# Two transformer blocks on one core: the second attention's probabilities with keys on the partitions

## The chip, the cores and the metric

The kernel runs on one core of a Trainium2 chip. The core has five engines that each work through their own queue in order: TensorE (PE) multiplies, with its weight loads shown apart as PEld; VectorE (DVE) and ScalarE (ACT) do element-wise work; GpSimd (POOL) does a little element-wise work here; SyncE (SP) issues DMAs. They meet by semaphores. The metric is the device time of one execution in microseconds; lower is better.

## What is computed

A batch of 2 sequences of 2048 rows by 512 passes through four stages, each with a layer norm and a residual; the context is 77 rows by 512 for each sequence.

```python
# stage 1: attention without heads over the 77 context rows
align = softmax(ex @ eother.T); x = x + tanh(g) * (align @ iother)
# stage 2: feed-forward with ternary weights, 512 -> 2048 -> 512, exact gelu
# stage 3: the second attention: 16 heads of 32, 77 keys
q = query @ Wq + bq; k, v = context @ Wkv + bkv
scores = einsum('bhid,bhjd->bhij', q, k) * 32 ** -0.5
scores = where(mask, -inf, scores)
out = einsum('bhij,bhjd->bhid', softmax(scores), v) @ Wout + bout
# stage 4: gated feed-forward with weights and inputs quantised to fp4 blocks
```

The change touches stage 3 alone, and the order of the work that runs beside it.

## The kernel before

The 4096 rows are taken in 8 groups of 512 (`GROUPS`), each of 4 tiles of 128 rows (`TILES`). Two groups are always in flight. `phase_a(g3, g1)` runs stage 3 of one group beside stage 1 of the next and the first 8 of its 16 up-projections ("ups", L1251) of stage 2. `phase_b(g, s4)` runs the rest of stage 2 of the next group, and its stage 3 queries, beside stage 4 of the first. So the kernel is: phase A and B of group 0 alone, seven periods of A and B with two groups each, and a last phase A with stage 3 alone followed by a last stage 4. A phase is a list of steps (A) or slots (B), written out for each engine: every engine has a function `attend(g, n)` that says what it does for stage 3 at step n of phase A, and `stage1(g, n)` for stage 1. Nothing is planned at run time: an engine takes its queue in this order and waits (`want(engine, name, group, count)`) where a semaphore isn't there yet. An operation that waits holds back all behind it on its engine.

Precision: an fp32 operand is split into a high and a low fp16 half, and a product takes three passes (high by high, high by low, low by high). The low half is made by a subtraction.

Stage 3 of a tile t has 4 chunks c of 4 heads; n = 4t + c is the step. For each chunk:

- PE `scores` (L1329): queries are the weights (128 features by 128 rows), keys of four heads stand side by side as a block-diagonal of 308 columns; three passes and one for the mask, into bank 4 or 5. The result has rows on partitions.
- DVE `row_max` (L967, L969): minus the maximum of each row and head.
- ACT `powers_of` (L543, L550): exp for each head by itself, 128 rows by 77 keys, with minus the maximum as bias, and the sum of the row as a by-product (an `ACTIVATION_READ_ACCUMULATOR` behind each).
- PE, two steps on (L1370): four transposes in fp32, so that keys are on the partitions, into bank 6 or 7. ACT copies the high half out (L561), DVE subtracts to make the low half (L988).
- PE, four steps on: 12 short products with the values into bank 2 (`vals1`).

For each tile: DVE takes the reciprocals of the sums (L993) and normalises into `on3` (L979); PE transposes it (L1380), ACT and DVE split it (L570, L998), PE multiplies by Wout (12 + 1 matmuls, `out3`), DVE adds the residual (L1005) and takes the statistics of stage 4 (L731). When tiles 0 and 1 are there (`VAR4_AT`), POOL takes a root (`root4`, L422, `rstd4`) and DVE normalises and quantises them as the input of stage 4 (`x4`, L914, then `quant_x4` in parts 0 to 4); tiles 2 and 3 follow at the start of phase B.

The scores of steps 0 and 1, their maxima and the first exp are made at the end of phase B, between the third and the fourth query chunk. The fourth quarter of the previous hidden tile is quantised around there as well: its last part (`quant4` part 4) comes in step 2 (`LATE_QUANT`), its transposing DMA from SP after it (`turn_h`, L354), and its down-projection `late_down` (L1308) in steps 4 to 7.

Stage 1 starts its four tiles at steps 0, 1, 6 and 7 (`START1`). Its output is normalised at step 16 (`NORM2_AT`) and transposed by PE at step 17 (`x_t(2, ...)`, L1207, L1220) into banks 0, 1, 4 and 5; ACT makes the high half (L490), DVE the low half (L768); ups 0 to 7 follow in steps 18 to 25. After each up ACT makes gelu twice and a square (L514, L517, L519) and POOL the low half (L443), in its phase B list.

## Time and profile before

| | us |
|---|---|
| median of 3 runs | 1691.92 |
| lowest and highest | 1691.38, 1700.05 |
| the profiled execution | 1697.49 |
| its span, first to last instruction | 1695.7 |
| PE busy | 1348.8 (80%) |
| DVE busy | 1365.5 (81%) |
| ACT busy | 702.5 (41%) |
| POOL busy | 265.1 (16%) |

The seven periods repeat closely. The one looked at below has the end of its phase B (queries) at 808 to 823 us, phase A from 823 to 898, and the next phase B from 898 on. In the chain of work "issue" is time without a releaser that the profile shows. A duration in the timeline includes the time in which the next instruction of the same engine already runs, so what one costs its engine is the distance between two starts.

### The profile page before, as it was taken

What the parts mean: (1) busy time and instruction counts of PE and PEld (TensorE: products, weight loads), DVE (VectorE), ACT (ScalarE), POOL (GpSimd) and SP (SyncE); (2) the same over time, 40 slices, a digit from 0 to 9 for tenths busy, and PEclk for the clock granted to TensorE, in tenths of its full rate; (3) what the DMA queues carried; (4) which work ended last, traced back from release to release, by engine and by line L of the source; (5) the groups of instructions that cost most, each with busy time, mean ns of one, the idle gap of its engine ahead of it and who ended that gap; (6) DMA issues with size and microseconds to landing.
All of it is one profiled execution on the core that took longest, in us unless ns stands there. A gap on an engine that the chain in (4) does not pass through costs nothing.

```text
span 1695.7 us, 22446 instructions
## 1 busy us (share of the span) xinstructions
PE 1348.8 (80%) x8120; PEld 700.3 (41%) x8120; DVE 1365.5 (81%) x2364; ACT 702.5 (41%) x2113; POOL 265.1 (16%) x205
## 2 busy tenths in 40 slices
PE   5053645889988998889889988899889988898775
PEld 4021213644454445434554445344644464344421
DVE  6998688877888787878887788688887888786786
ACT  2222303752365326641565146522763165514510
POOL 1102200032003300230014000320032002400000
PEclk9557867999999999999999999999999999998987
DMA  9264684034113231133103420341132310341012
GB/s 350 90 225 142 133 212 108 2 62 75 50 26 57 44 87 26 32 59 82 29 14 63 75 63 14 62 75 50 26 57 44 88 26 12 62 73 30 20 19 62
DMA packets 267429, 119.71 MB, mean 71 GB/s; under 512 B 244122, under 2 KB 244634, under 8 KB 265782
## 3 DMA queue, kind: packets, MB, share of 16 engines
q1 hardware_dynamic: 259158, 102.54, 26.7%
q10 hardware_dynamic: 8160, 15.73, 2.5%
q8 instruction: 65, 1.06, 0.3%
q14 instruction: 46, 0.38, 0.1%
HBM read 49.04 MB, written 8.39 MB: 34 GB/s over the span
## 4 chain that ended last, share of the span: by engine, by line
PE 41%; DVE 29%; ACT 5%; issue 4%; DMA 1%; POOL 1%; DVEq 0%; POOLq 0%; ACTq 0%
PE bank L1180 23%; PE bank L1280 8%; PE bank L1265 6%; DVE stats L731 3%; DVE amax L884 2%; DVE xt L768 2%; DVE pair L893 2%; DVE region L988 2%; PE bank L1370 2%; DVE hid L937 2%; ACT region L550 1%; PE bank L1313 1%; DVE pair L901 1%; DVE xb L914 1%; DVE pair L903 1%
## 5 line engine op out<-in xcount | busy, mean ns | idle before, releaser
L1265 PE MATMUL bank<-w_up,xt 128*128 128x512 fp8e4 x1024 | 246.9, 393 | 51.7 <-ACT region L517 37.3
L1280 PE MATMUL bank<-w_dn,region 128*128 128x512 fp8e4 x1024 | 235.9, 384 | 29.9 <-DMA region<-region 29.9
L443 POOL TENSOR_TENSOR region<-g,region 128x512 f16<-128x512 f32 x128 | 169.7, 1331 | 265.3 <-ACT region L517 257.4
L532 ACT ACTIVATE th<-bank,each 128x512 f32<-128x512 f32 x100 | 68.7, 687 | 331.0 <-PE bank L1180 322.9
L1265 PEld LDWEIGHTS bank<-w_up,xt 128*128 128x128 f16 x1024 | 102.3, 101 | 178.9 <-ACT region L517 38.3
L1180 PE MATMUL bank<-w_gate,xqt 128*128 128x512 bf16 x512 | 144.0, 407 | 36.0 <-DVE th L926 21.6
L550 ACT ACTIVATE region<-bank,nm 128x77 f32<-128x77 f32 x512 | 159.6, 338 | 21.7 <-DVE nm L969 20.5
L1280 PEld LDWEIGHTS bank<-w_dn,region 128*128 128x128 f16 x1024 | 101.4, 99 | 155.3 <-DMA region<-region 30.9
L1180 PE MATMUL bank<-w_gup,xqt 128*128 128x512 bf16 x512 | 140.6, 399 | 26.0 <-DVE hid L937 20.7
L514 ACT ACTIVATE g<-bank 128x512 f32<-128x512 f32 x128 | 76.4, 597 | 196.3 <-PE bank L1265 178.2
L1220 PE MATMUL bank<-ident,region 128*128 128x128 f32 x384 | 60.7, 310 | 81.6 <-DVE region L762 76.2
L490 ACT ACTIVATE xt<-bank 128x512 f16<-128x512 f32 x96 | 54.9, 605 | 158.8 <-PE bank L1220 158.7
L937 DVE TENSOR_TENSOR hid<-th,bank 128x512 f32<-128x512 f32 x92 | 63.0, 685 | 68.8 <-PE bank L1180 68.2
L550 ACT ACTIVATION_READ_ACCUMULATOR region<-bank,nm 128x1 f32 x512 | 112.1, 219 | 0.0
L561 ACT ACTIVATE region<-bank 77x512 f16<-77x512 f32 x128 | 77.5, 606 | 74.6 <-PE bank L1370 74.3
L1180 PE MATMUL bank<-w_down,hqt 128*128 128x512 bf16 x384 | 91.0, 392 | 13.5 <-DMA hqt<-pair 13.5
L1180 PE MATMUL bank<-w_o,region 128*128 128x512 f16 x384 | 91.1, 388 | 13.2 <-DVE region L998 13.2
L1180 PEld LDWEIGHTS bank<-w_gate,xqt 128*128 128x128 bf16 x512 | 48.6, 102 | 107.1 <-ACT th L532 32.2
L1180 PE MATMUL bank<-xt,w_q 128*128 128x512 f16 x384 | 89.2, 387 | 3.9 <-DVE xt L768 3.1
L1180 PEld LDWEIGHTS bank<-w_gup,xqt 128*128 128x128 bf16 x512 | 48.8, 103 | 105.2 <-DVE hid L937 41.8
L1220 PEld LDWEIGHTS bank<-ident,region 128*128 128x128 f32 x384 | 50.4, 159 | 95.5 <-issue 58.3
L1370 PE MATMUL bank<-ident,region 128*77 128x128 f32 x512 | 86.9, 295 | 2.1 <-DVE x L951 2.1
(211 smaller groups left out, 2525.1 us busy)
## 6 DMA issues: line engine op xcount, KB each, us to landing
out_x<-x ACTq DMA_DIRECT2D x16, 512.0 KB, 2.8
xin<-in_x ACTq DMA_DIRECT2D x14, 512.0 KB, 4.7
region<-in_w_up_t SPq DMA_DIRECT2D x1, 4096.0 KB, 14.0
hid<-in_gate_w SPq DMA_DIRECT2D x4, 1024.0 KB, 5.3
x<-in_gate_w SPq DMA_DIRECT2D x4, 1024.0 KB, 5.6
hid<-in_up_w SPq DMA_DIRECT2D x4, 1024.0 KB, 5.2
x<-in_up_w SPq DMA_DIRECT2D x4, 1024.0 KB, 5.7
hid<-in_down_w SPq DMA_DIRECT2D x4, 1024.0 KB, 4.9
```

Of the source, the lines that this page charges most:

```text
L443: eng.tensor_tensor(hn[1][:, t % 2, ns], g32[:, s % 2, :], hn[0][:, t % 2, ns], ALU.subtract).then_inc(sg["hl"], 1)
L490: eng.activation(xt[0][:, :, t * P:(t + 1) * P], state_bank(stage, t)[:, :].rearrange("p (k t) -> p k t", k=KD), ACT.Copy).then_inc(sg[f"x ...
L514: eng.activation(g32[:, s % 2, :], bank[s % 2][:, :], ACT.Gelu).then_inc(sg["g32"], 1)
L532: eng.activation(th[:, u % 2, :], bank[4][:, :], ACT.Silu, scale=cg[:, :]).then_inc(sg["th"], 1)
L550: last = eng.activation(p3[:, n % 2, j, :], bank[4 + n % 2][:, j * M:(j + 1) * M], ACT.Exp, bias=nm3[:, n % 2, j:j + 1], accum_out=rs3[:, ...
L561: eng.activation(pt3[0][0:M, m % 2], bank[6 + m % 2][0:M, :].rearrange("p (h t) -> p h t", h=HC), ACT.Copy).then_inc(sg["p3h"], 1)
L937: eng.tensor_tensor(buf[:, n * D:(n + 1) * D], th[:, u % 2, :], bank[5][:, :], ALU.mult).then_inc(sg["hid"], 1)
L1180: last = mm(out, lhs, rhs, start=(n == 0), stop=(n == len(pairs) - 1))
L1220: last = tr(state_bank(stage, t)[:, k * P:(k + 1) * P], xn[:, t, k * P:(k + 1) * P], ident[:, :])
L1265: last = mm(bank[s % 2][:, :], xt[i][:, k, ts], w_up[:, k, n * D:(n + 1) * D], start=(k == 0 and i == 0), stop=(k == KD - 1 and i == 1))
L1280: last = mm(bank[2 + t % 2][:, :], ht[i][:, t % 2, f, :], w_dn[:, f, :], start=(f == 0 and i == 0), stop=(f == KF - 1 and i == 1))
L1370: last = tr(bank[6 + m % 2][0:M, j * P:(j + 1) * P], p3[:, m % 2, j, :], ident[:, :])
```

## The change

Stage 3 no longer transposes its probabilities; it makes them with keys on the partitions. This needs each row's maximum before the exponent, on the other axis, so that the scores are made twice.

- Queries and keys of each head are stacked three times 32 rows high (high, high, low against high, low, high), so that one pass over 96 rows takes the place of three: `qs` and `kst`. The stacking is done by DMAs from SP: `stack_q`, 24 DMAs of 64 KB for each group, in two halves of 12 with their own semaphores; it stands between `turn_h(g, 2)` and `turn_h(g, 3)` in SP's list. The keys are stacked once by 12 DMAs.
- First pass, `scores`: the mask (308 columns) and four products of 77 columns, always into bank 4, so it waits for the maxima of the step before. The maxima of a tile (`nm3`) are copied once more beside themselves (`nmc`), transposed by PE in one operation (`turn_max`), and split by ACT and DVE into `mx`.
- Second pass, `shifted_scores`, 5 steps later (`LAG_S`): for each head keys as weights (77 columns), 128 rows moving, and a short product that adds minus the maximum; into bank 6 or 7.
- ACT `powers_of`: two exps over 77 by 512 in place of four exps, four accumulator reads and a copy. The mask of a key is now a bias column `mcol`.
- The low half of the probabilities is made by POOL (`low3`) in place of DVE.
- `weigh`: values carry a column of ones, so that the sums come out of the product; 12 matmuls as before, into two banks. Normalising is done in two halves for each tile.
- Nothing of stage 3's scores is done in phase B any more. `stack_q` waits for the query halves there.
- Order: `LATE_QUANT` goes from step 2 to 0, `late_down` from 4..7 to 3..6. The stage 2 transposes use banks 0 and 1 alone, in steps 17 and 18, and ups 0 to 7 go from steps 18..25 to 19..26. The output of a tile comes later: for tile t the product with Wout goes from step 4t + 11 to 4t + 14. `VAR4_AT` goes from 17 to 20. POOL's low halves of ups 0 to 7 and its roots are now in phase A's list by step, and `root4(g, 1)` is at the head of phase B, behind the low half of up 7 (before: behind that of up 6).

```diff
-LATE_QUANT, LATE_DOWN, LATE_OUT = 2, (4, 5, 6, 7), 8
+LATE_QUANT, LATE_DOWN, LATE_OUT = 0, (3, 4, 5, 6), 7
-UP_AT = {T2_AT + 1 + i: i for i in range(UPS_A)}
+UP_AT = {T2_AT + 2 + i: i for i in range(UPS_A)}
+LAG_MX, LAG_S = 1, 5
+LAG_V = LAG_S + 2
+LAG_ON, LAG_OT, LAG_OTL, LAG_OUT, LAG_X3 = (LAG_V + i for i in (1, 2, 3, 4, 5))
+VAR4_AT = NC + NC - 1 + LAG_X3 + 1
...
+            def stack_q(g):
+                want_ht(sp, g, 2)
+                want_ht(sp, g, 3)
+                for a in range(2):
+                    cs = slice(2 * a, 2 * a + 2)
+                    for r, made, i in ((0, "qh", 0), (1, "qh", 0), (2, "ql", 1)):
+                        want(sp, made, g, 2 * a + 2)
+                        for j in range(HC):
+                            dst = qs[HD * r:HD * (r + 1), :, :].rearrange("p (c j) t -> p c j t", j=HC)[:, cs, j, :]
+                            sp.dma_start(dst, qt[i][HD * j:HD * (j + 1), cs, :]).then_inc(sg[f"stacked{a}"], 16)
...
+                for n in range(STEPS):
...
+                    if g3 is not None and 0 <= n - LAG_S < TILES * NC:
+                        low3(g3, n - LAG_S)
+                    if g3 is not None and n == VAR4_AT:
+                        root4(g3, 0)
+                    if g1 is not None and n in UP_AT:
+                        low(g1, UP_AT[n])
...
-                for j in range(HC):
-                    h = HC * c + j
-                    last = eng.activation(p3[:, n % 2, j, :], bank[4 + n % 2][:, j * M:(j + 1) * M], ACT.Exp,
-                                          bias=nm3[:, n % 2, j:j + 1], accum_out=rs3[:, t % 2, h:h + 1])
-                last.then_inc(sg["p3"], 1)
+                want(act, "s3", g, m + 1)
+                if m >= 2:
+                    want(act, "p3l", g, m - 1)
+                eng.activation(p32[0:M, m % 2, :], bank[6 + m % 2][0:M, :], ACT.Exp, bias=mcol[:, b:b + 1])
+                if m >= 2:
+                    want(act, "o3", g, m - 1)
+                eng.activation(pt3[0][0:M, m % 2, :], bank[6 + m % 2][0:M, :], ACT.Exp,
+                               bias=mcol[:, b:b + 1]).then_inc(sg["p3"], 1)
...
-                elif s < 2:
-                    want(pe, "xl2", g, s + 1)
+                elif s < 2:
+                    want(pe, "xl2", g, s + 3)
...
-                product(bank[4 + n % 2][:, 0:HC * M],
-                        [(qt[0][:, c, sl], k_hi), (qt[0][:, c, sl], k_lo), (qt[1][:, c, sl], k_hi),
-                         (row_one_b[:, :], mrow[:, b].rearrange("p h m -> p (h m)"))]).then_inc(sg["sc3"], 1)
+                if n:
+                    want(pe, "nm3", g, n)
+                at = bank[4]
+                mm(at[:, 0:HC * M], row_one_b[:, :], mrow[:, b].rearrange("p h m -> p (h m)"), start=True, stop=False)
+                for j in range(HC):
+                    last = mm(at[:, j * M:(j + 1) * M], qs[:, HC * c + j, t * P:(t + 1) * P],
+                              kst[:, HC * c + j, b * M:(b + 1) * M], start=False, stop=(j == HC - 1))
...
+            def shifted_scores(g, m):
...
+                if c == 0:
+                    want(pe, "ml", g, t + 1)
+                if m >= 2:
+                    want(pe, "p3", g, m - 1)
...
+                    last = product(bank[6 + m % 2][0:M, j * P:(j + 1) * P],
+                                   [(kst[:, h, b * M:(b + 1) * M], qs[:, h, t * P:(t + 1) * P]),
+                                    (sel[0:MXR, h:h + 1].to_broadcast([MXR, M]), mx[0:MXR, t % 2, :])])
...
+            def weigh(g, m):
...
+                want(pe, "p3l", g, m + 1)
...
+            def attend(g, n):
+                t = tile_at(n, LAG_MX)
+                if t is not None:
+                    turn_max(g, t)
+                if n < TILES * NC:
+                    scores(g, n)
+                if 0 <= n - LAG_S < TILES * NC:
+                    shifted_scores(g, n - LAG_S)
+                if 0 <= n - LAG_V < TILES * NC:
+                    weigh(g, n - LAG_V)
```

## Rows read from the trace of the kernel before

**Rows 1.** Busy time of each engine (instructions) in three stretches: us, engines, granted clock, DMA
```profile
823.40:834.00 10.60, 6.33 (x54) 5.21 (x53) 10.39 (x15) 7.12 (x33) 0.00 (x0) 0.69 0.17 32
834.00:871.40 37.40, 33.65 (x374) 23.64 (x372) 31.20 (x77) 27.30 (x130) 2.33 (x2) 1.00 0.07 21
871.40:906.40 35.00, 28.13 (x158) 13.82 (x158) 27.62 (x54) 21.34 (x47) 13.59 (x12) 0.99 0.37 69
```

**Rows 2.** Chain that ended last, same period: start us, us, engine, tile, line
```profile
843.71 0.59 DVE region L988
...
897.64 1.16 POOL region L443
...
899.49 1.84 DVE xb L914 x2
...
905.71 0.69 DVE th L926
```

**Rows 3.** Timeline of PE: start us, us, line, out<-in, shape, count, idle and releaser
```profile
829.69 0.96 PE L1180 MATMUL bank<-keys,xt 128*128 128x77 f16 x12 [4.27 <-DVE xt L768]
...
847.02 0.59 PE L1180 MATMUL bank<-keys,xt 128*128 128x77 f16 x12
847.45 0.20 PE L1180 MATMUL bank<-crow,row_one 128*128 128x77 f16 x1
...
859.99 0.56 PE L1180 MATMUL bank<-keys,region 128*128 128x308 f16 x3
860.39 0.29 PE L1180 MATMUL bank<-mrow,row_one_b 128*128 128x308 bf16 x1
860.52 0.46 PE L1180 MATMUL bank<-vals,region 77*128 77x32 f16 x12
860.82 0.64 PE L1370 MATMUL bank<-ident,region 128*77 128x128 f32 x4
861.30 0.60 PE L1380 MATMUL bank<-ident,acc 128*128 128x128 f32 x4
...
871.47 2.02 PE L1220 MATMUL bank<-ident,region 128*128 128x128 f32 x16 [0.83 <-DVE region L762]
```

**Rows 4.** Timeline of ACT, and for L538 min/median/max ns of one
```profile
817.98 0.68 ACT L540 ACTIVATE region<-bank,bq 128x512 f16<-128x512 f32 x1
...
821.27 1.28 ACT L550 ACT_TABLE_LOAD   x1
822.57 0.33 ACT L550 ACTIVATE region<-bank,nm 128x77 f32<-128x77 f32 x1
...
822.88 0.32 ACT L550 ACTIVATE region<-bank,nm 128x77 f32<-128x77 f32 x1
...
L538 ACT ACTIVATE region<-bank,bq x32: 687/688/707, 281.5 to 1549.4; 128x512 f32<-128x512 f32 x32
```

**Rows 5.** DVE: two lines with min/median/max ns, then two of its timeline
```profile
L988 DVE TENSOR_TENSOR region<-bank,region x128: 674/677/686, 295.1 to 1590.8; 77x512 f16<-77x512 f32 x128
...
L969 DVE TENSOR_REDUCE nm<-bank x128: 455/469/480, 288.6 to 1585.3; 128x4 f32<-128x308 f32 x128
...
877.52 1.00 DVE L914 TENSOR_SCALAR xb<-x,mv,rstd 128x512 f32<-128x512 f32 x2
...
889.28 0.68 DVE L998 TENSOR_TENSOR region<-bank,region 128x512 f16<-128x512 f32 x1
```

**Rows 6.** SP issuing DMAs at the start; a store with us to landing
```profile
0.72 0.45 SPq L269 DMA_DIRECT2D xb<-in_ctx_t  x1
1.23 0.49 SPq L269 DMA_DIRECT2D region<-in_w_t  x1
...
out_x<-x ACTq DMA_DIRECT2D x16, 512.0 KB, 2.8
```

**Rows 7.** POOL's L443 and DVE's L914: min/median/max ns of one
```profile
L443 POOL TENSOR_TENSOR region<-g,region x128: 1149/1159/2136, 142.5 to 1477.9; 128x512 f16<-128x512 f32 x128
...
L914 DVE TENSOR_SCALAR xb<-x,mv,rstd x32: 533/540/1373, 339.4 to 1610.3; 128x512 f32<-128x512 f32 x32
```

297 lines of the change are left out of this document (152 added, 145 removed).

## The prediction

> **What bounds the kernel now.** I read the busy times first, then the chain of waits, then the timelines of one period, then single lines. PE and DVE are each busy four fifths of the span, ACT well under half. The stretch from the end of the queries to the first gate product that waits for quantised work (823.4 to 906.4 us) is what the change edits. Its windows [rows 1] show three regimes. In the first 10.6 us DVE is busy 10.39 and PE 6.33, at a granted clock of 0.69, so partly at 1.2 instead of 2.4 GHz after it had idled. In the next 37.4 PE (33.65) and DVE (31.20) are both nearly full and ACT has 27.30. In the last 35.0 PE (28.13) and DVE (27.62) hand over to each other. The chain [rows 2] says who ends last: in the middle it changes between PE and DVE, and the low half of the probabilities (L988) lies on it; near the end it goes low half of an up (POOL), root, x4 on DVE from 899.49, hidden tile at 905.71, and PE's gate product at 906.44. So ACT, which the change relieves most, ends last almost nowhere. What counts is PE, DVE and the hand-overs.
>
> **What each step costs its engine.** PE: from the distances of starts [rows 3] three score passes take 0.40 us and the mask 0.13; the 12 value products 0.30; four transposes 0.48; together 1.31 for each of 16 steps. After: the mask 0.13 and four products of 77 columns, which cost 0.036 each where 12 took 0.43 [rows 3], so 0.28 for the first pass. The second pass is 8 products of 128 columns, half of them 48 rows deep, with 77 columns of weights. No row shows these in fp16. From below they cost 0.036 each (the 77-column products), from above 0.12 each (the transposes of the same two sizes, in fp32), so 0.29 to 0.96; I take 0.43, 0.053 each: 128 columns at the rate at which the 308 columns took 0.13. Values 0.30 as before. Sum 1.01, and 4 times about 0.12 for `turn_max`: PE saves 4.3 us a period, 1.0 of it in phase B.
>
> DVE: L988 leaves, 16 times 0.60 (0.677 with 0.08 of overlap) [rows 5], 9.6 us. The halves of the normalising, copies of maxima and the low half of `mx` add some 0.6 a tile. Net 7 us less. `row_max` stays at 0.47 [rows 5], but PE now waits for it in every step, since bank 4 is the only one. ACT: four exps at 0.31 apart [rows 4] and a copy (1.7 us) become two exps of 77 by 512 with a bias column. Bounds: 0.33 [rows 4] and 0.69, a 128 by 512 one with a bias column (L538) [rows 4]; I take 0.6, so 1.2 and 16 times 0.5 us less. POOL: 16 new low halves of 77 by 512; nearest is L443, 1.16 us at the median [rows 7]: 18.6 us more on an idle engine.
>
> **The sum, as a walk through one period.** Times are those of the period before; what is said of after is shifted to the same start.
>
> Start. The second query chunk's high half is there at 818.66 [rows 4]. From then SP can issue. Two issues at the start of the kernel are 0.51 apart [rows 6]; 24 need 12.2 us, so the last of the second half goes out at 830.4. A landing takes up to the 2.8 us of a 512 KB store [rows 6]; nothing says that 64 KB are much quicker, so `stacked1` is there at 833.2 (bounds 831, no time but the issue, and 836, a crowded queue). Queued behind it on PE, in step 2: the scores, then stage 1's first scores, then all else. Those started at 829.69 before, after PE had waited 4.27 us for DVE [rows 3]. After: 833.5. **3.8 us lost**; the old 4.27 us covers the rest. `turn_h(g, 3)` now stands behind 24 issues on SP, but its data is made at about 830, so it leaves at 831, as before, and `late_down` waits at most 1 us.
>
> Middle, up to the stage 2 transposes, which start at 871.47 [rows 3]: 41.8 us before. After, PE's work from step 2 to 16 is 25.6 us: 0.28 a step, 0.43 from step 5, 0.30 from step 7, stage 1, `late_down`, and one product with Wout (2.9 us) where there were two: the other now comes behind the transposes. DVE has 24 us. Taking in each step the longer of the two gives 32; perfect overlap gives 26. The engines run about a step apart, so I take 30.5: transposes at 864.0, **7.5 us earlier**.
>
> Tail, first part. The second product with Wout now lies between the two pairs of transposes (to 869.6), and the second pair uses banks 0 and 1 again, so it waits for DVE's low halves: 870.4. On ACT the copies of that pair stand ahead of the exp of chunk 13, so exps 13 and 14 end at 873.6. Then up 0 wants gelu and chunk 15 wants exp: a table is loaded for gelu, for exp and for gelu again, 1.28 us each [rows 4], where one load did. Load and three operations of up 0, 3.2 us; load and two exps, 2.5: 879.2. On POOL the low half of chunk 15 (1.16) and then the root of tiles 0 and 1 are queued behind it: 881.1. The first half of x4 begins on DVE at 881.2 instead of 877.52 [rows 5]. **So 3.7 later**, though the transposes were 7.5 earlier: ACT, no limit before, becomes one through its order.
>
> Rule against row: the trace has the next exp 0.02 us behind the load's end [rows 4], so a load costs 1.28. The Trainium skill ("ScalarE: Activation LUTs", What ACT_TABLE_LOAD costs) gives about 1.38 us of draining beside it, 2.66 in all. By it two more loads would cost 2.8 us more a period, 19 us in the kernel; the row decides and the sum is without it.
>
> Tail, second part. From there DVE works without a pause to the low half before the last product with Wout (L998, 889.28 [rows 5]): 11.8 us before, now 1.2 more since the last part of the quantising goes ahead of it: 894.2. Product 2.8, up 7 1.7: 898.7. Its second gelu 1.2, low half 1.16, root 0.7: x4's second half at 901.7 instead of 899.49 [rows 2]. Before, the root stood behind up 6's low half, so an up more is now ahead of it. The 7 us from there to PE's gate product are DVE's and do not change: 908.7 instead of 906.44. **2.2 us later a period.** The 1.0 us saved on PE in phase B is in this, since phase A starts that much earlier.
>
> To this come frictions, bounded by 0 and 4 us a period. The clock: PE is idle in two long pieces before 833, and the slow stretch of 4.5 us after the old one cost some 2; I take 0.7. POOL against DVE: x4's L914 takes 540 ns at the median and 1373 at most [rows 7], the latter beside POOL's low halves; 16 more of these now run beside the stage 2 normalising (four wide operations and some small ones) and the copies of maxima; I take 0.6. Weights of 77 columns at the upper bound would add up to 0.5 a step, much of it under DVE. Sum 3.5 a period.
>
> Kernel: 7 times 3.5 is 24.5. The last phase A has no ups, so no second table load, and keeps the gain of the middle: 3.8 - 7.5 + 0.7, 3.0 less. The prologue's key splitting gets shorter on DVE, but DVE waits there next for the sums of the ternary weights, so I count nothing; if that cover is thin it is 1 to 5 us of gain. Together 21.5 more: 1697.5 + 21.5 = 1719.0 for the profiled execution; it lies 5.6 above the median, so the median goes from 1691.9 to **1713.4**.
>
> **The rivals.** (1) ACT's order does not hold the tail. If exp 15 and the root are done by 875, when the statistics of tile 1 are, the tail runs by PE alone: 28.4 us of work from 864 and 1.5 of waits, up 7's end at 893.9 instead of 898.0, and after the extra low half still 3 us before the old time. Seven periods and the last phase: 24 less, 1668. For it: ACT has 13 us of idle in the last window [rows 1]; against it: its queue is in order. This is the other side, and it decides by whether the first x4 starts before about 878.
>
> (2) The terms cancel: the middle comes out at 27 instead of 30.5 or the stacking lands at 831. Within 8 us of the old time, about 1692. For it: L988 lay on the chain [rows 2] and is gone altogether.
>
> (3) The new short loops fail to overlap: one bank for the first pass makes PE and DVE alternate (0.28 + 0.47 and two hand-overs in every step), and POOL's low halves block DVE's wide operations and are blocked. Then the middle takes 34.5, x4 is hit too, 7.5 a period: 52 - 3, 1741. For it: the 1373 and 2136 ns [rows 7]. By the Trainium skill ("SBUF — State Buffer", on the port pair that VectorE and GpSimd share) the later of the two stands still for the other's whole instruction.
>
> **How the numbers follow.** Forecast 0.35 (by itself 1700 to 1727), rival 1 0.25, rival 2 0.18, rival 3 0.22. The range goes from rival 1 to rival 3, 1668 to 1742, since neither can be left out. About 0.5% (8.5 us) is what a measurement of this kernel can tell from no change. Faster by more 0.27, within 0.18, slower by more 0.55.
>
> **What would show it.** In the new trace: SP's 24 issues 0.5 apart and stage 1's first scores at 10 us behind the queries' end or later (right), or at 7 (wrong). The stretch from those to the stage 2 transposes near 30 us. Five table loads a period instead of three. x4's first half waiting for POOL's root, not for its statistics. x4's second half behind up 7's low half. Second-pass products near 0.05 apart. L914 and the stage 2 normalising longer than 0.54. If DVE is still full from the transposes to x4, the forecast of the tail is wrong; if DMA landings are not what PE waits for in step 2, that of the start is.

## The result, and the profile after

| | before | after |
|---|---|---|
| median, us | 1691.65 | 1922.73 |
| lowest and highest | 1688.60, 1700.05 | 1920.95, 1924.73 |
| the profiled execution's span | 1695.7 | 1922.9 |
| PE busy | 1348.8 (80%) | 1533.8 (80%) |
| DVE busy | 1365.5 (81%) | 1318.5 (69%) |
| ACT busy | 702.5 (41%) | 664.8 (35%) |
| POOL busy | 265.1 (16%) | 408.4 (21%) |

The ratio is 1.136, 95% interval 1.132 to 1.139 (four runs each): 13.6% slower, where 1713.4 (1668 to 1742) was forecast. The sign was right, the size was not. The kernel before, run again beside the experiments, had medians of 1690.8 to 1698.0, so a difference of under some 7 us between two kernels says little by itself. DVE, ACT and POOL moved about as expected; PE, which was to become 4.3 us lighter in each period, was busy for 185 us more in all.

The chain that ended last, after:

```profile
PE 52%; DVE 24%; SPq 7%; ACT 6%; issue 5%; DMA 3%; POOL 2%; DVEq 0%; POOLq 0%; ACTq 0%
```

The costliest groups that are new (busy us, mean ns, idle time before and its releaser):

```profile
L1232 PE MATMUL bank<-mx,sel 48*77 48x128 bf16 x512 | 141.4, 276 | 0.0
L1232 PE MATMUL bank<-qs,kst 96*77 96x128 f16 x512 | 139.9, 273 | 0.0
...
L1385 PE MATMUL bank<-mrow,row_one_b 128*128 128x308 bf16 x128 | 49.4, 386 | 83.5 <-DMA qs<-region 82.4
```

The first two lines are the second pass. Their busy times can't be added, since the products overlap; by the starts, a step's eight products hold PE for 1.64 us on average, 210 us in all 128 steps, where 0.43 a step, 55 us, was forecast. The third is where PE waits for the stacked queries, 82.4 us in all.

Windows of one period after (from the queries' end to the first gate product):

```profile
512.10:525.60 13.50, 3.54 (x24) 2.70 (x24) 8.06 (x10) 3.74 (x5) 0.00 (x0) 0.82 0.49 107
525.60:575.40 49.80, 49.11 (x423) 30.77 (x420) 29.21 (x76) 20.90 (x46) 16.09 (x14) 0.74 0.07 20
575.40:595.10 19.70, 19.23 (x143) 11.22 (x144) 9.77 (x21) 12.59 (x21) 6.43 (x6) 0.83 0.00 1
595.10:613.50 18.40, 16.32 (x79) 7.49 (x77) 13.03 (x27) 12.09 (x29) 8.44 (x7) 1.00 0.37 69
```

The second line is the stretch from stage 1's first scores to the stage 2 transposes. The same stretch, in the same period, of the kernel before and of k96, an experiment below:

```profile
469.60:511.40 41.80, 37.41 (x410) 26.73 (x411) 35.59 (x84) 30.00 (x144) 2.33 (x2) 0.97 0.11 27
503.50:539.40 35.90, 31.60 (x422) 23.28 (x419) 27.91 (x76) 20.77 (x46) 16.28 (x15) 0.88 0.10 27
```

After the change PE is busy there for 49.11 of 49.80 us and the granted clock is 0.74, where it was 0.97. DVE has 29.21: it is not the limit there. PE alone sets this stretch, and it does so with the second pass, whose products start 0.178 us apart at 2.4 GHz and 0.25 at 1.2 (timeline of PE: start, us, line, tile):

```profile
539.42 0.25 PE L1232 MATMUL bank<-qs,kst 96*77 96x128 f16 x1
539.61 0.25 PE L1232 MATMUL bank<-mx,sel 48*77 48x128 bf16 x1
539.78 0.25 PE L1232 MATMUL bank<-qs,kst 96*77 96x128 f16 x1
...
559.25 0.33 PE L1232 MATMUL bank<-qs,kst 96*77 96x128 f16 x1
559.50 0.32 PE L1232 MATMUL bank<-mx,sel 48*77 48x128 bf16 x1
```

Where the 227.2 us between the two spans lie, by the starts of PE's queries: 9.8 before the first (276.2 to 286.0), 39.8 in the first phase A and B with two groups (172.3 to 212.1), 153.2 in the six periods that follow (181.0 to 206.5), 24.4 in the last phase A and stage 4 (161.5 to 185.9). The forecast had priced the first period like the six, at 3.5, the prologue at nothing and the last phase at 3.0 less.

To compare kernels I cut the six periods at the same five events and take means. The columns: from the last query product to the first scores of stage 1; from there to the root of stage 2's variances (POOL, `sdev`); from there to the first half of x4; from there to the first gate product; from there to the last query product of the next period (phase B with its queries). This table is worked out from the start times of those operations in each trace, and its entries are good to 0.1:

| kernel (median of its runs) | start | middle | to x4 | to gate | phase B | period |
|---|---|---|---|---|---|---|
| before (1691.7) | 6.5 | 36.9 | 11.2 | 22.9 | 103.4 | 181.0 |
| after (1922.7) | 14.1 | 38.4 | 31.7 | 18.8 | 103.5 | 206.5 |
| k96, equal heights (1807.0) | 14.0 | 28.2 | 27.6 | 18.8 | 104.2 | 192.8 |
| k96ord, ACT's order too (1780.1) | 14.1 | 28.0 | 25.7 | 18.6 | 103.0 | 189.4 |
| k96all, two queues and prologue too (1742.5) | 10.0 | 28.6 | 26.2 | 18.6 | 103.1 | 186.4 |
| lag4 (1784.5) | 10.1 | 39.9 | 17.7 | 20.4 | 103.5 | 191.7 |
| tail2 (1747.3) | 9.9 | 28.6 | 23.6 | 20.2 | 104.2 | 186.6 |
| allswap (1763.7) | 9.9 | 28.6 | 27.9 | 18.6 | 103.9 | 188.9 |
| alldve (1745.7) | 10.2 | 31.1 | 23.0 | 18.6 | 102.8 | 185.6 |

### The profile page after: what moved, and what is told of

Read it like the earlier page. It is cut to its first block, busy times and chain, and to the rows that moved or that the text cites. A ratio compares the mean times of both kernels' runs of the same rounds, so it can differ in the third digit from the quotient of the medians.

```text
span 1922.9 us, 23112 instructions
## 1 busy us (share of the span) xinstructions
PE 1533.8 (80%) x8792; PEld 780.1 (41%) x8792; DVE 1318.5 (69%) x2345; ACT 664.8 (35%) x1263; POOL 408.4 (21%) x333
## 3 DMA queue, kind: packets, MB, share of 16 engines
q1 hardware_dynamic: 276334, 115.60, 27.1%
q8 instruction: 70, 1.15, 0.2%
## 4 chain that ended last, share of the span: by engine, by line
PE 52%; DVE 24%; SPq 7%; ACT 6%; issue 5%; DMA 3%; POOL 2%; DVEq 0%; POOLq 0%; ACTq 0%
PE bank L1232 29%; PE bank L1328 7%; PE bank L1313 7%; SPq L374 5%; DVE amax L934 2%; PE bank L1359 2%; DVE hid L939 2%; PE bank L1269 1%; DVE hid L987 1%; DVE stats L781 1%; DVE xt L818 1%; DMA w_gup<-in_w_dn_t 1%; DVE pair L958 1%; SPq L341 1%; DVE region L812 1%
## 5 line engine op out<-in xcount | busy, mean ns | idle before, releaser
L463 POOL TENSOR_TENSOR region<-region 77x512 f16<-77x512 f32 x128 | 147.8, 1155 | 372.0 <-ACT region L604 372.0
L473 POOL TENSOR_TENSOR region<-g,region 128x512 f16<-128x512 f32 x128 | 165.3, 1295 | 278.7 <-ACT region L567 278.1
L1232 PE MATMUL bank<-w_gup,xqt 128*128 128x512 bf16 x512 | 140.4, 399 | 26.2 <-DVE hid L987 20.9
L601 ACT ACTIVATE region<-bank,mcol 77x512 f32<-77x512 f32 x128 | 87.4, 683 | 197.8 <-PE bank L1232 197.7
L1022 DVE TENSOR_REDUCE nm<-bank 128x4 f32<-128x308 f32 x128 | 60.7, 474 | 121.8 <-PE bank L1387 121.2
L538 ACT ACTIVATE xt<-bank 128x512 f16<-128x512 f32 x96 | 55.2, 595 | 251.5 <-PE bank L1269 251.1
L1232 PE MATMUL bank<-mx,sel 48*77 48x128 bf16 x512 | 141.4, 276 | 0.0
L1232 PE MATMUL bank<-qs,kst 96*77 96x128 f16 x512 | 139.9, 273 | 0.0
L1269 PE MATMUL bank<-ident,region 128*128 128x128 f32 x384 | 74.2, 346 | 78.2 <-DVE region L812 70.6
L1232 PE MATMUL bank<-w_o,region 128*128 128x512 f16 x384 | 121.9, 483 | 2.5 <-DVE region L1053 2.5
L1385 PE MATMUL bank<-mrow,row_one_b 128*128 128x308 bf16 x128 | 49.4, 386 | 83.5 <-DMA qs<-region 82.4
L1269 PEld LDWEIGHTS bank<-ident,region 128*128 128x128 f32 x384 | 58.1, 180 | 91.1 <-issue 60.5
```

Of the source, the lines that this page charges most:

```text
L463: eng.tensor_tensor(pt3[1][0:M, m % 2, :], p32[0:M, m % 2, :], pt3[0][0:M, m % 2, :], ALU.subtract).then_inc(sg["p3l"], 1)
L473: eng.tensor_tensor(hn[1][:, t % 2, ns], g32[:, s % 2, :], hn[0][:, t % 2, ns], ALU.subtract).then_inc(sg["hl"], 1)
L601: eng.activation(p32[0:M, m % 2, :], bank[6 + m % 2][0:M, :], ACT.Exp, bias=mcol[:, b:b + 1])
L1022: eng.tensor_reduce(nm3[:, t % 2, HC * c:HC * (c + 1)], bank[4][:, 0:HC * M].rearrange("p (h m) -> p h m", h=HC), AX.X, ALU.max, negate=Tr ...
L1232: last = mm(out, lhs, rhs, start=(n == 0), stop=(n == len(pairs) - 1))
L1269: last = tr(state_bank(stage, t)[:, k * P:(k + 1) * P], xn[:, t, k * P:(k + 1) * P], ident[:, :])
```

## The experiments

### Why 0.178 us

Three theories: weights narrower than 128 columns load slowly (1); the change of height between 96 and 48 rows costs (2); the second product of a pair waits for the first (3). Three kernels tell them apart.

**wide.** 128 columns of weights.

```diff
-                    last = product(bank[6 + m % 2][0:M, j * P:(j + 1) * P],
-                                   [(kst[:, h, b * M:(b + 1) * M], qs[:, h, t * P:(t + 1) * P]),
-                                    (sel[0:MXR, h:h + 1].to_broadcast([MXR, M]), mx[0:MXR, t % 2, :])])
+                    last = product(bank[6 + m % 2][:, j * P:(j + 1) * P],
+                                   [(kst[:, h, b * M:b * M + P], qs[:, h, t * P:(t + 1) * P]),
+                                    (sel[0:MXR, h:h + 1].to_broadcast([MXR, P]), mx[0:MXR, t % 2, :])])
```

> The second pass's products have 128 columns of weights in place of 77 (the 51 further output partitions are not used). After: each of the 8 products of a step started 0.178 us behind the one before at 2.4 GHz, 0.255 at 1.2 GHz. Theory 1, the weights are what costs: a product with weights narrower than 128 columns whose weights change each time starts only when they are in; with 128 the distance falls to 0.05 to 0.07, a step to 0.5 us, some 0.9 less in each of 128 steps, 115 us of PE; DVE takes over some of it, so 1750 to 1820 us. Theory 2, the change of height between 96 and 48 rows costs, and theory 3, the second product of a pair waits for the first's accumulation: distance stays at 0.178 and the time at 1922.

Measured: 1901.5 us. The distance is 0.160:

```profile
537.08 0.23 PE L1233 MATMUL bank<-mx,sel 48*128 48x128 bf16 x1
537.24 0.23 PE L1233 MATMUL bank<-qs,kst 96*128 96x128 f16 x1
537.40 0.23 PE L1233 MATMUL bank<-mx,sel 48*128 48x128 bf16 x1
```

Theory 1 had asked for 0.05 to 0.07 and for 100 to 170 us; it gets 0.018 of the 0.11 or more, and 21 us (the two runs are 14 apart).

**nomx.** Without the maxima product, so the result is not that of the kernel; exp is taken of 0.05 times the score (not shown in the cut) to stay finite.

```diff
-                                   [(kst[:, h, b * M:(b + 1) * M], qs[:, h, t * P:(t + 1) * P]),
-                                    (sel[0:MXR, h:h + 1].to_broadcast([MXR, M]), mx[0:MXR, t % 2, :])])
+                                   [(kst[:, h, b * M:(b + 1) * M], qs[:, h, t * P:(t + 1) * P])])
```

> Left out: the product that adds minus the maximum in the second pass, so 4 products a step in place of 8; exp is taken of 0.05 times the score to stay finite. Theory 1 (narrow weights cost): the four that stay are still 0.17 to 0.18 apart, a step falls by 0.7 us, 90 us of PE in all, the time to 1830 to 1860. Theory 2 (changing height) and theory 3 (waiting for the accumulation): they close up to 0.05 to 0.07, a step falls by 1.2, the time to 1770 to 1800.

Measured: 1798.5 us, 124 less than after. That is what theories 2 and 3 gave, at the upper end of their range, and more than the 63 to 93 of theory 1. Half the products are gone here, so it can't settle the matter alone; the four that stay start 0.056 apart.

**k96.** The maxima product 96 rows deep, the added rows zero; still 77 columns, and the pair still accumulates.

```diff
-                                    (sel[0:MXR, h:h + 1].to_broadcast([MXR, M]), mx[0:MXR, t % 2, :])])
+                                    (sel[0:3 * HD, h:h + 1].to_broadcast([3 * HD, M]), mx[0:3 * HD, t % 2, :])])
```

> The product that adds minus the maximum is made 96 rows deep like the other (rows of zeros), so that no height changes between products; the weights stay at 77 columns. Theory 2 (the change of height costs): distance falls from 0.178 to 0.05 to 0.07, the time to 1750 to 1820. Theories 1 and 3: distance 0.178 and 1922 us as before.

Measured: 1807.0 us. One height in the source takes 115.7 us off. The distance is 0.056, as the forecast had assumed:

```profile
537.13 0.22 PE L1232 MATMUL bank<-qs,kst 96*77 96x128 f16 x1
537.18 0.22 PE L1232 MATMUL bank<-mx,sel 96*77 96x128 bf16 x1
537.24 0.22 PE L1232 MATMUL bank<-qs,kst 96*77 96x128 f16 x1
```

8 products in 128 steps, each 0.122 closer, are 125 us at 2.4 GHz; by the starts, with the stretches at 1.2 GHz, the second pass goes from 210 to 65 us. 115.7 arrive. Theory 3 is out (the pair accumulates as before), theory 1 too (77 columns as before), and so is the alternation of fp16 and bf16, which k96 keeps. More rows, more multiplications, less time.

The weight loads show what the change of height does. In the kernel after, each load starts together with its own product (compare 539.61 and 539.78 above); in k96 it starts together with the product before it, 0.054 ahead of its own. Kernel after, then k96:

```profile
539.60 0.11 PEld L1232 LDWEIGHTS bank<-mx,sel 48*77 48x77 bf16 x1
539.78 0.11 PEld L1232 LDWEIGHTS bank<-qs,kst 96*77 96x77 f16 x1
...
537.13 0.12 PEld L1232 LDWEIGHTS bank<-mx,sel 96*77 96x77 bf16 x1
537.18 0.12 PEld L1232 LDWEIGHTS bank<-qs,kst 96*77 96x77 f16 x1
```

So at a change of height the load no longer runs ahead beside the product before. That is why the width mattered in **wide**: there the load is in the open.

**k96wide.** Both edits.

```diff
+                                   [(kst[:, h, b * M:b * M + P], qs[:, h, t * P:(t + 1) * P]),
+                                    (sel[0:3 * HD, h:h + 1].to_broadcast([3 * HD, P]), mx[0:3 * HD, t % 2, :])])
```

> Equal heights as in the 1807 us kernel, and 128 columns of weights in place of 77 in the second pass. With alternating heights the wider weights brought the distance of products from 0.178 to 0.160 us and the time down by 21. Theory H, it is the height alone: with equal heights 77 columns already run at 0.056 and 128 columns do too, 1803 to 1811. Theory W, narrow weights have a cost of their own: the distance falls below 0.05, 5 to 15 us less.

Measured: 1806.2 us. With equal heights the width is worth nothing that these runs show; it shortened only the wait at a change of height.

**k96half.** Height 96 for the maxima of two heads, 48 for those of two.

```diff
+                                    (sel[0:(MXR if j >= 2 else 3 * HD), h:h + 1].to_broadcast([MXR if j >= 2 else 3 * HD, M]),
+                                     mx[0:(MXR if j >= 2 else 3 * HD), t % 2, :])])
```

> The changed kernel, with the maxima product 96 rows deep for two of the four heads of a chunk and 48 for the other two: four changes of height a step where there were eight (and where there are none in the equal-height kernel). Theory, each change of height costs about 0.12 us: the first four products of a step 0.056 apart, the last four near 0.178, and half of the 116 us comes back: 1860 to 1872. Rival, mixing at all keeps the pipeline slow, or removing half of it is hidden by DVE: 1900 or more, or below 1830.

Measured: 1845.9 us, 76.8 less than after and 39 more than k96: two thirds come back, where theory had half (1860 to 1872). A step of its trace (the first five products stand 0.06 apart, two of them are left out):

```profile
548.20 0.22 PE L1232 MATMUL bank<-qs,kst 96*77 96x128 f16 x1
...
548.37 0.22 PE L1232 MATMUL bank<-mx,sel 96*77 96x128 bf16 x1
548.42 0.22 PE L1232 MATMUL bank<-qs,kst 96*77 96x128 f16 x1
548.57 0.24 PE L1232 MATMUL bank<-mx,sel 48*77 48x128 bf16 x1
548.75 0.25 PE L1232 MATMUL bank<-qs,kst 96*77 96x128 f16 x1
548.93 0.24 PE L1232 MATMUL bank<-mx,sel 48*77 48x128 bf16 x1
549.11 0.19 PE L1428 MATMUL bank<-vals,region 77*128 77x33 f16 x1
```

Only the distances with a change between them are long (0.15, 0.18, 0.18, and 0.18 to the value product of 77 rows), four in place of eight. In PE's time at 2.4 GHz that is half: a step's median is 1.40 us in the kernel after, 0.91 here and 0.45 in k96. What comes back beyond the half goes with the clock: the middle of the same period runs at 0.88 here already, as in k96, where the kernel after has 0.74.

**k80.** The maxima product 80 rows deep beside 96.

```diff
+                                    (sel[0:80, h:h + 1].to_broadcast([80, M]), mx[0:80, t % 2, :])])
```

> The changed kernel, with the maxima product 80 rows deep (32 rows of zeros) beside the other's 96. Theory E, any inequality of height costs: 0.178 us apart and 1922. Theory C, heights fall in classes (the mask's 128 rows followed by 96, and 77 rows in the value products, cost nothing that the trace shows) and 48 lies in a lower one than 96: 0.056 apart and 1807.

Measured: 1807.1 us, and the products stand close (0.058):

```profile
540.10 0.22 PE L1232 MATMUL bank<-mx,sel 80*77 80x128 bf16 x1
540.16 0.22 PE L1232 MATMUL bank<-qs,kst 96*77 96x128 f16 x1
```

So unequal heights are not the cost: 80 beside 96 is free, 48 beside 96 is not. Heights fall into classes; where between 48 and 80 the border lies was not tried. The Trainium skill ("TensorEngine Tiling (Array Packing)", Tiling Modes) names tiling modes of 128, 64 and 32 rows, and says that changing the mode, not only the tile, drains TensorE. It doesn't say that a product of 48 rows takes another mode by itself; that these are the same thing is my reading. The traces agree with it: 48 beside 96 is 0.178 us apart, 80 or 96 beside 96 is 0.056 to 0.058. The section gives no price for the drain; here the change costs 0.122 us with 77 columns of weights.

### The start

**twoq.** A third of the stacking from ACT's queue.

```diff
-                    for r, made, i in ((0, "qh", 0), (1, "qh", 0), (2, "ql", 1)):
+                    for r, made, i in ((0, "qh", 0), (2, "ql", 1)):
...
+                if c % 2:
+                    want(act, "qh", g, c + 1)
+                    cs = slice(c - 1, c + 1)
+                    for j in range(HC):
+                        dst = qs[HD:2 * HD, :, :].rearrange("p (c j) t -> p c j t", j=HC)[:, cs, j, :]
+                        eng.dma_start(dst, qt[0][HD * j:HD * (j + 1), cs, :]).then_inc(sg[f"stacked{c // 2}"], 16)
```

> 8 of the 24 stacking DMAs are issued from ACT's queue, behind the two query chunks that they need; SP issues 16. Theory A, SP's issuing (24 in 15.3 us, 0.64 each) sets the start: the last stacked half is there 3 to 5 us earlier, waits of PE for the stacked queries fall from 82 us to about 45, the time by 25 to 40 us, to 1885 to 1900. Theory B, it is the low halves of the queries or the transfers themselves that come last: waits stay near 80 and the time within 5 us of 1922, or longer by what ACT loses.

Measured: 1903.4 us, 19 less; PE's waits for `qs` fall from 82.4 to 27.1. Theory A holds for the start, which falls from 14.1 to 9.8 us, but the time falls by less than the waits (its range was 1885 to 1900). In the table's terms the middle gave 1.5 of the 4.2 us back, and PE's waits for the row maxima of the step before rose from 1.1 to 23.7 us in the kernel.

**k96q.** The same on equal heights.

> On top of the equal heights (1807 us): 8 of the 24 stacking DMAs leave from ACT's queue. On the changed kernel alone it took 19 us off, of 55 that PE had waited less for qs. If the start stands by itself in the sum, 19 again, 1788; if with a faster middle PE is less the bound there and ACT's 8 issues delay what it does next, under 10.

Measured: 1775.1 us, 32 less: more than alone, the opposite of what I had thought possible. The six periods are 3.4 us shorter each (4.2 at the start, some 0.5 given back in each of the next three stretches, 0.8 won in phase B), 20 in all; the first is 7 shorter (191.2 to 184.2), and the last phase A with stage 4 is 6 shorter (171.9 to 165.6). Why two queues are worth more here than alone is not shown.

SP's side of it in the kernel after:

```profile
508.34 15.29 SPq L374 DMA_DIRECT2D qs<-region  x24
...
517.42 0.44 PE L1385 MATMUL bank<-mrow,row_one_b 128*128 128x308 bf16 x1 [5.29 <-DMA qs<-region]
...
525.11 0.44 PE L1385 MATMUL bank<-mrow,row_one_b 128*128 128x308 bf16 x1 [4.67 <-DMA qs<-region]
```

24 issues take 15.3 us, 0.64 each, and a landing 2.0. The two waits of PE, in steps 0 and 2, are those for `stacked0` and `stacked1`.

### The tail

**k96ord.** ACT makes exp 15 ahead of up 0; POOL makes its low half and the root of tiles 0 and 1 ahead of the low half of up 0.

```diff
-                if 0 <= n - LAG_S < TILES * NC:
+                if 0 <= n - LAG_S < TILES * NC - 1:
                     powers_of(g, n - LAG_S)
+                if n - LAG_S == TILES * NC - 2:
+                    powers_of(g, n - LAG_S + 1)
...
                     if g1 is not None and n in UP_AT:
-                        low(g1, UP_AT[n])
+                        if g3 is None or UP_AT[n] > 1:
+                            low(g1, UP_AT[n])
+                        elif UP_AT[n] == 1:
+                            low(g1, 0)
+                            low(g1, 1)
```

> On top of the equal heights (1807 us): ACT makes the exps of chunk 15 ahead of up 0, and POOL makes low half 15 and the root of tiles 0 and 1 ahead of the low half of up 0. Theory: ACT's order in the tail costs what the prediction said. Two of five table loads a period go (2.6 us of ACT); x4's first half, in the equal-height kernel at 558.76 behind a root that ended at 558.72, starts 4 us earlier (exps done at 552.6, low half 553.8, root 554.5), and most of that reaches the gate products: 3 to 4 a period, 1780 to 1786. Rival: what comes later, the product with Wout for tiles 2 and 3 and the second half of x4, sets the first gate product, and up 0 now starts 2 us later: no gain within 5 us.

Measured: 1780.1 us, 26.9 less. The order of two queues costs 3.4 us a period (192.8 to 189.4), as theory had it. But x4 comes only 1.9 us earlier behind the root of stage 2, where 4 was expected; 1.3 of the rest is in phase B. The trace of after shows the order as foretold, ACT first, then POOL, then x4:

```profile
587.59 1.28 ACT L564 ACT_TABLE_LOAD   x1
588.89 0.60 ACT L564 ACTIVATE g<-bank 128x512 f32<-128x512 f32 x1
...
590.60 1.28 ACT L601 ACT_TABLE_LOAD   x1
591.89 0.68 ACT L601 ACTIVATE region<-bank,mcol 77x512 f32<-77x512 f32 x1
592.48 0.67 ACT L604 ACTIVATE region<-bank,mcol 77x512 f16<-77x512 f32 x1
...
593.65 1.28 ACT L564 ACT_TABLE_LOAD   x1
```

```profile
593.23 1.15 POOL L463 TENSOR_TENSOR region<-region 77x512 f16<-77x512 f32 x1 [2.02 <-ACT region L604]
594.34 0.69 POOL L457 TENSOR_TENSOR rstd<-ve,powers 128x2 f32<-128x2 f32 x1
595.07 1.00 DVE L964 TENSOR_SCALAR xb<-x,mv,rstd 128x512 f32<-128x512 f32 x2 [0.71 <-POOL rstd L457]
```

**k96dve3.** The low half of the probabilities back on DVE.

```diff
-                    if g3 is not None and 0 <= n - LAG_S < TILES * NC:
-                        low3(g3, n - LAG_S)
...
+                m = n - LAG_S - 1
+                if 0 <= m < TILES * NC:
+                    want(dve, "p3", g, m + 1)
+                    eng.tensor_tensor(pt3[1][0:M, m % 2, :], p32[0:M, m % 2, :], pt3[0][0:M, m % 2, :],
+                                      ALU.subtract).then_inc(sg["p3l"], 1)
```

> On top of the equal heights (1807 us): the low half of the probabilities is made by DVE, as in the kernel before, in place of POOL (0.6 us, 16 times a period). Theory P, POOL's 1.15 us in the chain and its blocking of DVE (the stage 2 normalising L812 3.64 us for four against 1.91) cost more than DVE's time: faster, by up to 3 a period, 1785 to 1800. Theory D, DVE is full in the middle and the move to POOL was worth what the prediction gave it: slower by 4 to 8 a period, 1835 to 1865.

Measured: 1795.8 us, 11.3 less. The 9.6 us of DVE work a period that the prediction had booked as the change's largest relief were worth less than nothing. By the starts in its trace the middle is 2.2 us a period longer than in k96 (30.3), so DVE's work does count there; x4 comes 3.8 earlier behind the root of stage 2 (23.8), where POOL's 1.15 us stood in the chain and its low halves beside DVE's.

**k96all.** k96ord, k96q, and in the prologue POOL's reduction of the weights' maxima ahead of the low halves of ups 0 to 7.

```diff
+                    if g3 is None and n == min(UP_AT):
+                        pool.wait_ge(sm["wmax_all"], 3)
+                        eng.partition_all_reduce(red[:, 2:5], wmax[:, :], P, RMAX).then_inc(sm["wsum_all"], 1)
```

> Equal heights, the reordered tail, the issues on two queues, and in the prologue POOL's reduction of the weights' maxima ahead of the low halves of ups 0 to 7, where it was before the change. If the three losses add up: 1807 - 19 (queues) - 25 (tail) - 8 (prologue) = 1755, still 3.4% over the kernel before, since the start keeps some 4 us a period and the tail stays longer. If a common bound (PE or DVE in the middle) takes over, 1775 to 1785.

Measured: 1742.5 us, 64.5 less than k96, where 26.9 and 31.9 were the parts: they add up and leave 6 for the prologue, whose queries start at 277.7 instead of 284.9. The expectation had 1755, with the queues at their 19 us. It is the fastest version found, and still 2.7% (2.3 to 3.1) over the kernel before. Its span is 44.1 us longer: 5.4 in each of six periods, 8.2 in the first, 1.5 and 1.9 at the two ends.

Of the 5.4, the start is still 3.5 (10.0 against 6.5), and it is no longer mainly the DMAs. PE waits 26.6 us for stacked queries and 36.9 for row maxima in this kernel, where k96 has 82.0 and 13.6. The first pass has one bank, so step 1's scores wait for the maxima of step 0, and DVE comes to them only behind the quantising at the end of phase B:

```profile
474.97 0.30 PE L1398 MATMUL bank<-mrow,row_one_b 128*128 128x308 bf16 x1 [2.74 <-DMA qs<-region]
479.86 0.44 PE L1398 MATMUL bank<-mrow,row_one_b 128*128 128x308 bf16 x1 [3.98 <-DVE nm L1035]
...
476.08 1.22 DVE L956 TENSOR_SCALAR pair<-hid 128x2048 f16<-128x2048 bf16 x1
479.33 0.47 DVE L1035 TENSOR_REDUCE nm<-bank 128x4 f32<-128x308 f32 x1
```

No run takes this wait away.

**alldve.** k96all with the low half on DVE.

> The kernel with equal heights, reordered tail, two queues and the mended prologue (1742 us), and the low half of the probabilities on DVE in place of POOL. By itself that took 11 us off the equal-height kernel. Theory P, POOL's 1.15 us lie in the chain to x4 and its blocking of DVE counts also here: 10 to 15 less, 1728 to 1732. Theory O, the reordered tail has taken the same gain already: within 5 of 1742.

Measured: 1745.7 us, no difference within the spread of its runs (1736.6 to 1755.1). Theory O: the middle loses 2.5 us and x4 comes 3.2 earlier. This trace and that of k96all also price POOL's effect on DVE. The stage 2 normalising in both, k96all first:

```profile
L825 DVE TENSOR_SCALAR region<-xin,mv,rn 128x512 f32<-128x512 f32 x32 | 21.3, 727 | 0.3
```

```profile
L823 DVE TENSOR_SCALAR region<-xin,mv,rn 128x512 f32<-128x512 f32 x32 | 15.3, 543 | 0.3
```

543 ns without POOL's low halves beside it, 727 with; in the kernel after it was 860. The Trainium skill ("SBUF — State Buffer", on the port pair that VectorE and GpSimd share) lets the later of the two stand still. The trace agrees in sign; for these 32 operations it is 6 us in the kernel.

### What is left, and three reorderings that failed

**lag4.** The second pass 4 steps behind the first.

```diff
-LAG_MX, LAG_S = 1, 5
+LAG_MX, LAG_S = 1, 4
```

> Equal heights, two queues and the mended prologue, and the second pass 4 steps behind the first in place of 5, so that all of stage 3 behind it comes a step earlier; exp 15 then stands ahead of up 0 by itself. PE now waits for the split maxima in the step in which they are turned. Theory L, the depth of the two-pass pipeline is what still stands between 1742 and the kernel before (from the root of stage 2 to x4 26 us in place of 11): x4's first half comes 2 to 4 us earlier, 1715 to 1730. Theory M, the waits for the maxima in four steps (each 1 us) and PE's work take it back: 1738 to 1750.

Measured: 1784.5 us, 42 more. Theory L is right about the tail: x4 comes 17.7 us behind the root of stage 2 in place of 26.2. Theory M is right about the sum, and more so than I had priced it: the middle takes 39.9 in place of 28.6. PE waits in four steps for the maxima that DVE and ACT have just split, and the wait grows with what is ahead of the split in DVE's queue:

```profile
493.60 0.33 PE L1239 MATMUL bank<-qs,kst 96*77 96x128 f16 x1 [0.89 <-DVE mx L1055]
...
506.17 0.25 PE L1239 MATMUL bank<-qs,kst 96*77 96x128 f16 x1 [2.28 <-DVE mx L1055]
```

These waits are 42.4 us in the kernel, and the granted clock of the middle is 0.79 where k96all has 0.87.

**allswap.** PE makes the second pair of the stage 2 transposes ahead of the product with Wout of tile 1.

```diff
+                    if g1 is not None and n == T2_AT + 1:
+                        stage1(g1, n)
                     if g3 is not None:
                         attend(g3, n)
-                    if g1 is not None:
+                    if g1 is not None and n != T2_AT + 1:
                         stage1(g1, n)
```

> The 1742 us kernel, and PE makes the second pair of the stage 2 transposes ahead of the product with Wout of tile 1, not behind it; in its trace the second pair waited for that product, from 521.96 to 526.33, while DVE and ACT stood still for 4.5 us. Theory S, the place of the product costs: the pair starts at about 523.2, ups 0 and 1 and all behind them 2 to 3 us earlier, 1722 to 1732. Theory T, x4 waits for the product and not for the ups: it comes 1 us later than before, 1740 to 1752.

Measured: 1763.7 us, 21 more. Theory T, and more than its 1752: the transposes come 3.8 us earlier behind the queries in the period looked at, but the product stands behind a wait now (1.78 us for DVE's low half) and comes 3.6 later, and with it the first up (2.3) and, on average, x4 (1.7).

**tail2.** k96all, and ACT copies the output of tile 2 ahead of up 0. The trace of k96all had given the reason (DVE):

```profile
535.52 0.69 DVE L1066 TENSOR_TENSOR region<-bank,region 128x512 f16<-128x512 f32 x1 [3.27 <-ACT region L634]
536.13 1.85 DVE L977 TENSOR_SCALAR xb<-x,mv,rstd 128x512 f32<-128x512 f32 x2
```

```diff
-                t = tile_at(n, LAG_OT)
+                t = 2 if n == LAG_OT + 10 else None if n == LAG_OT + 11 else tile_at(n, LAG_OT)
```

> The 1742 us kernel, and ACT copies the turned output of tile 2 ahead of up 0. In the trace of that kernel DVE stood still for 3.27 us before x4, not for POOL's root (done at 533.87) but for this copy (534.89), which ACT made behind the table load and up 0. Theory Q, the order of ACT's queue still sets x4: the copy comes at about 532, x4 2 us earlier and the product with Wout of tile 2 as well: 12 to 20 less, 1722 to 1730. Rival R, the two failed reorderings were no accident, since ups 0 and 1 start later by what x4 gains and phase B takes it back: within 5 of 1742.

Measured: 1747.3 us. x4 comes 2.6 us earlier, as theory Q says, and the stretches behind it take nearly 3 us longer, as rival R says. DVE in tail2:

```profile
536.52 0.69 DVE L1066 TENSOR_TENSOR region<-bank,region 128x512 f16<-128x512 f32 x1 [0.26 <-ACT region L634]
537.92 1.00 DVE L977 TENSOR_SCALAR xb<-x,mv,rstd 128x512 f32<-128x512 f32 x2 [0.71 <-POOL rstd L457]
```

The 3.27 us of waiting are gone and the time is not: the chain of the ups is as long as that of x4, and ACT serves both. Moving one ahead of the other exchanges the two. What remains against the kernel before, beside the 3.5 us of the start, is not one wait but the depth of the pipeline: the output of tile 1, by the lags of the source, is added in step 19 where it was in step 16, so the first x4 stands 15 us further behind the root of stage 2 (26.2 against 11.2), while the middle and the stretch to the gate give back 8.3 and 4.3. So behind the start the depth costs 2 to 3 us a period on balance. That the depth is the cause is argued from lag4's 17.7 and from the lags; a version with the old depth and without the new waits was not tried.

## Why the prediction was wrong, by its steps

**The second pass** is the step that failed. It was priced by rows of other shapes [rows 3], 0.053 us a product with an upper bound of 0.12. It measured 0.178: a step of 1.42 us in place of 0.43, above the bound of 0.96. The bound was the fault more than the value. Each row it came from was a run of products of one height, and nothing in [rows 3] is under 77 rows high; the new work alternates between 96 and 48. A rival was open to the prediction, though not its price: the rule on tiling modes of the Trainium skill, told under k80, bears on the 48 rows of this change, and it was not weighed. "The transposes of the same two sizes" was true of each product and silent on their sequence. The price 0.053 itself was right, to 0.003, once the sequence was uniform (k96). This is 115.7 of the 209 us by which the forecast missed; k96 at 1807 would still have lain 94 over it, outside the range. In the prediction's own stretches, as means of the six periods, changes against before:

| stretch | forecast | k96 | after |
|---|---|---|---|
| queries to stage 1's first scores | +3.8 | +7.6 | +7.6 |
| from there to the stage 2 transposes | -11.3 | -5.7 | +8.2 |
| from there to the first half of x4 | +11.2 | +13.4 | +13.9 |
| from there to the gate | -1.5 | -4.2 | -4.2 |
| phase B, and frictions | +1.3 | +0.8 | +0.1 |
| period | +3.5 | +11.9 | +25.5 |

The entries are rounded one by one.

**The start** was mis-sized: 3.8 us later was forecast, 7.6 measured. The mechanism is as described. The issue distance is 0.64, not the 0.51 of [rows 6], which makes 3.1 us over 24: the two rows were loads from memory, these are copies from one tile to another, and nothing in the text bounded the difference. The first issue stood 3.5 us ahead of the last query product (508.34 against 511.8), where the walk had 4.5. The landing, 2.0, was under the 2.8 taken.

**The middle**, here from stage 1's first scores to the stage 2 transposes, some 5 to 12 us more than the table's column. The walk had it shrink from 41.8 to 30.5 us, so that the transposes came 7.5 earlier in spite of the late start. In the kernel after it takes 50.1, under PE's load. With equal heights it takes 36.3: the sign was right, half of the size came, and the transposes stand 1.9 us later behind the queries than before. In the period shown, k96 has PE busy for 31.60 of 35.90 us at a granted clock of 0.88, where the walk had 25.6 of work and took 30.5; how much of the gap is the clock and how much a hand-over is not shown.

**Tail, part 1.** The mechanism is confirmed line by line: five table loads a period, exp 15 behind up 0, root behind its low half, x4 behind the root [rows 5 has the old start]. The size was a little short: with equal heights x4 stands 19.4 us behind the transposes, 13.4 more than before, where the walk gave 11.2 more (the 3.7 by which x4 was to be late and the 7.5 by which the rest was to be early). The walk had DVE and ACT go on without a pause between the pairs of transposes. In k96 they stand still for 4.4 and 5.4 us, since the product with Wout between the pairs takes 4.25 in place of 2.8:

```profile
540.75 1.12 PE L1269 MATMUL bank<-ident,region 128*128 128x128 f32 x4 [0.19 <-DVE region L812]
...
542.96 4.25 PE L1232 MATMUL bank<-w_o,region 128*128 128x512 f16 x12
```

PE had idled 1.44 and 0.19 us shortly before, and the second pass's products behind it stand 0.107 apart in place of 0.056: the clock was at 1.2 GHz there and for much of the product.

**Tail, part 2.** The stretch from x4 to the gate was to be 1.5 shorter (3.7 late, then 2.2); it is 4.2 shorter in the six periods. x4's second half does wait for up 7's low half and the root behind it (POOL 613.06 and 614.18, x4 614.91).

**The frictions** had been put at 1.3 us a period, mostly clock. The normalising took 860 ns in each of four operations where 543 is what it takes without POOL's low halves beside it, 1.3 us a period (in k96 it is 726); 0.6 was taken for all of that kind. The clock cost more than its 0.7 and not where I had put it, behind the idle pieces before stage 1's first scores: the middle ran at 0.74 while PE was busy all the time.

**What was counted at nothing or as a gain.** "The prologue 0": 9.8 us, since POOL's reduction of the weights' maxima had come behind eight low halves in its queue, and DVE waited 12.6 us for it. The text had looked at DVE's work there and not at what else the moved list of POOL was ahead of. "The last phase A ... 3.0 less": with stage 4, +10.4 with equal heights and +1.9 in k96all; the sum 3.8 - 7.5 + 0.7 also counts the late start twice, since the 7.5 has it already. And the first period: +18.9 with equal heights, where 3.5 was taken. Its old start was only 3.2 us long in place of 6.5, so the new one, 13.9 as in all others, costs 10.6 there; the stretch to x4 costs 17.3.

**The rivals.** Rival 3 named the right stretch, the middle, and a reason that is not the main one: with one bank and POOL as they are, equal heights take the middle from 50.1 to 36.3 us. The one bank does cost once the DMAs are quicker (36.9 us of PE's waits in k96all). Its 1741 is by chance that of k96all. Rival 1 is refuted: with ACT's order mended x4 still comes 25.7 us behind the root of stage 2, where it was 11.2. The likeliest reason is the depth, which no part of the text had priced as such. Rival 2 never came near.

**The rule on table loads.** The forecast took 1.28 us and set aside the 1.38 of draining from the Trainium skill ("ScalarE: Activation LUTs", What ACT_TABLE_LOAD costs). The trace agrees with the row: load at 590.60 for 1.28, next exp at 591.89. Two loads, the exchange of up 0 and exp 15, and POOL's order together were worth 3.4 us a period.

## What to carry to other kernels

A price read from a trace holds for a sequence, not for an instruction: ask what stands next to the new operation, and if no row shows that neighbourhood, say that there is no upper bound, or measure it. Where short products alternate with taller ones, try padding them with zeros to the height of their neighbours first; 48 rows of zeros gave 6% of the kernel here. And where a change makes a pipeline deeper by three steps, price the depth at the place where the last result is needed; emptying single waits behind it (tail2, allswap) or taking a step out of it (lag4) only moves them.

## What the hardware showed that I had not expected

- Products that alternate between 96 and 48 rows start 0.178 us apart with 77 columns of weights and 0.160 with 128; 96 and 96, 0.056, and 96 and 80, 0.058. In the first case a weight load starts 0.002 ahead of its own product (0.004 with 128 columns), in the others 0.054 to 0.057 ahead, beside the product before it.
- In the stretch in which PE was busy 49.11 of 49.80 us with such products, the granted clock was 0.74; in the same stretch of the kernel before, with 37.41 of 41.80 busy, it was 0.97, and in k96, with 31.60 of 35.90, 0.88. In these traces a PE that the profile shows as full is not one that keeps the clock.
- 24 copies of 64 KB leave SP's queue 0.64 us apart, and ACT's 0.65 (medians); splitting them over both took 32 us off the kernel with equal heights.
